# Attention and gated FFN on one core: where q's squares are transposed and summed, and three shifts in the order of work

## The reference

```python
xn = (x - mean) / sqrt(var + 1e-5)
q = rmsnorm(xn @ Wq.T) * q_norm_w      # 32 heads of 128
k = rmsnorm(xn @ Wk.T) * k_norm_w      # 8 groups of 128, 4 heads each
v = xn @ Wv.T
scores = q @ k.T / sqrt(128) + slope[h] * (s - t)   # causal, masked above the diagonal
s = concat_heads(softmax(scores) @ v) @ Wo.T
f = (silu(xn @ gate) * (xn @ up)) @ down            # hidden size 1792
# gate, up, down: integers, (w - zero) * scale per 128 rows
out = x + s * silu(f)
```

## Time and profile before

| | |
|---|---|
| three runs | 1301.31, 1301.42, 1301.54 us; median 1301.42 |
| the profiled execution | 1302.0 us, its span 1300.2 us |
| granted TensorE clock | full (2.4 GHz level) in all 40 slices |
| PE busy | 1281.2 us, 99% of the span |
| DVE busy | 972.3 us, 75% |
| POOL busy | 711.4 us, 55% |
| ACT busy | 650.8 us, 50% |
| DMA | 62.08 MB, mean 48 GB/s |

### The profile page before, as it was taken

How to read it: one execution, slowest core, us unless ns; L and a number is a source line. 1 busy time by engine, 2 the same in 40 slices (tenths; PEclk the granted TensorE clock), 3 DMA queues, 4 the chain that set the end, 5 groups by cost and what they waited for, 6 DMA issues and landing times.

```text
span 1300.2 us, 21057 instructions
## 1 busy us (share of the span) xinstructions
PE 1281.2 (99%) x7141; PEld 1099.9 (85%) x7141; DVE 972.3 (75%) x2089; ACT 650.8 (50%) x1433; POOL 711.4 (55%) x758
## 2 busy tenths in 40 slices
PE   8999999999999999999999999999999999999998
PEld 7888888888888888888888888888888888888887
DVE  6555555578888777877787778777877787778887
ACT  4322222355565555555555555555555555555552
POOL 4855555535555455545554555455545554555486
PEclk9999999999999999999999999999999999999999
DMA  6554555110010000000100000001000000000211
GB/s 187 160 143 130 128 129 130 31 74 17 17 34 17 17 18 33 18 17 17 33 18 17 17 33 17 17 17 34 17 17 18 33 17 17 17 17 17 98 57 66
DMA packets 31965, 62.08 MB, mean 48 GB/s; under 512 B 3840, under 2 KB 4096, under 8 KB 31744
## 3 DMA queue, kind: packets, MB, share of 16 engines
q1 hardware_dynamic: 31872, 60.88, 16.2%
HBM read 56.67 MB, written 4.19 MB: 47 GB/s over the span
## 4 chain that ended last, share of the span: by engine, by line
PE 89%; DVE 6%; ACT 2%; issue 2%; POOL 1%; DMA 0%; DVEq 0%; POOLq 0%
PE O L1088 31%; PE O L1149 13%; PE S L1668 12%; PE T L1109 10%; PE S L1128 5%; PE S L1131 5%; PE S L1129 5%; DVE pb L840 2%; PE T L1171 2%; PE O L1682 1%; PE T L1682 1%; PE O L1684 1%; PE T L1684 1%; PE O L1683 1%; PE T L1683 1%
## 5 line engine op out<-in xcount | busy, mean ns | idle before, releaser
L437 POOL TENSOR_TENSOR pb<-rel,coef 128x1024 f32<-128x1024 f32 (+7 forms) x256 | 293.2, 1160 | 139.9 <-PE T L1109 134.6
L579 ACT ACTIVATE pb<-pb,low 128x1024 f32<-128x1024 f32 (+7 forms) x256 | 198.9, 777 | 182.4 <-DVE low L840 180.5
L569 ACT ACTIVATE pt_h<-T 128x512 fp32r<-128x512 f32 (+3 forms) x384 | 185.0, 486 | 119.0 <-PE T L1109 115.8
L824 DVE TENSOR_TENSOR pt_l<-T,pt_h 128x512 fp32r<-128x512 f32 (+3 forms) x384 | 209.7, 549 | 43.1 <-ACT pt_h L569 43.0
L840 DVE CUSTOM_DVE_ANT_0 pb<-S,pb,ninv 128x1024 f32<-128x1024 f32 (+7 forms) x256 | 207.4, 810 | 36.8 <-PE S L1131 31.9
L1109 PE MATMUL T<-ident,pb 128*128 128x128 f32 x1152 | 188.9, 273 | 10.6 <-DVE ssum L869 4.7
L849 DVE TENSOR_SCALAR pb<-pb,rinv 128x1024 f32<-128x1024 f32 (+7 forms) x256 | 174.5, 682 | 9.0
L1109 PEld LDWEIGHTS T<-ident,pb 128*128 128x128 f32 x1152 | 140.5, 140 | 47.9 <-issue 13.9
L1128 PE MATMUL S<-kT_h,q_h 128*128 128x512 f32 (+2 forms) x384 | 141.5, 369 | 0.0
L1149 PE MATMUL O<-pt_h,v_h 128*128 128x512 f32 (+2 forms) x384 | 140.7, 366 | 0.1
L414 POOL TENSOR_TENSOR inv<-ms,cst 128x4 f32<-128x4 f32 x64 | 76.3, 1192 | 112.3 <-DVE ms L872 112.3
(11 more groups left out here) (177 smaller groups left out, 2899.3 us busy)
## 6 DMA issues: line engine op xcount, KB each, us to landing
wq_in<-in_wq SPq DMA_DIRECT2D x32, 256.0 KB, 2.8
wo_in<-in_wo SPq DMA_DIRECT2D x32, 256.0 KB, 2.6
stage<-in_wkv SPq DMA_DIRECT2D x8, 512.0 KB, 4.4
pb<-in_gate_w SPq DMA_DIRECT2D x14, 256.0 KB, 2.7
pb<-in_gate_z SPq DMA_DIRECT2D x14, 256.0 KB, 3.6
pb<-in_gate_s SPq DMA_DIRECT2D x14, 256.0 KB, 5.1
pb<-in_up_w SPq DMA_DIRECT2D x14, 256.0 KB, 5.3
pb<-in_up_z SPq DMA_DIRECT2D x14, 256.0 KB, 6.2
```

The costliest lines, as they stand in the source:

```text
L437: g_.tensor_tensor(pbuf(idx, t), rel[:, TOK - w:TOK], coef[:, t:t + 1].to_broadcast([P, w]), ALU.mult).then_inc(bias_ready, 1)
L569: a_.activation(pt_lot(pt_h, t, n), bank[:, 0:m * P].rearrange("p (k w) -> p k w", w=P), ACT.Copy).then_inc(tr_hi, 1)
L579: a_.activation(pbuf(idx, t), pbuf(idx, t), ACT.Exp, bias=low[:, idx:idx + 1], scale=-1.0, accum_out=rsum[:, idx:idx + 1]).then_inc(exps_r ...
L824: v_.tensor_tensor(pt_lot(pt_l, t, n), bank[:, 0:m * P].rearrange("p (k w) -> p k w", w=P), f(pt_lot(pt_h, t, n)), ALU.subtract).then_inc( ...
```

## The change

Half 0's squares no longer take part in the turns of the transpose banks.

- For heads 1 to 31, PE transposes them into the first bank of S[0] (`SQ_BANK`) with `squares_of_half_0`, which waits for q's squares and for logits 0 of this head (`logits_ready >= 8h + 1`), and raises a semaphore of its own, `sq_tr`. DVE's `mean_sq0` sums from there and raises `sq_sum`. Scores 2 gets a second wait, for `sq_sum`. The place among PE's work is the same.
- `PARTS` has 13 parts, and the bank of a part is that of its running number (`part_bank`).
- In the first and the last group, at j = 1 to 3, DVE sums in front of q_lo, not behind it. At j = 0 and in the steady groups the sum keeps its place.
- In heads 0 and 1, q_lo of the next head's qc1 moves behind the low part (4,1) and logits 5.
- In the prologue the transposes of x's tiles 6 and 7 stand in first_kv(4), not in first_kv(5).
- SP's wait in head 31 is for `sq_tr`.

```diff
-PARTS = ["ss0"] + LOTS[:LOTS.index((3, 0))] + ["ss1"] + LOTS[LOTS.index((3, 0)):]
-LN_PARTS = QT + 1
+PARTS = LOTS[:LOTS.index((3, 0))] + ["ss1"] + LOTS[LOTS.index((3, 0)):]
+LN_PARTS = QT + 2
+def part_bank(part):
+    return (part + 1) % 2
...
+    SQ_BANK = S[0][:, 0:CH]
...
-                    sp.wait_ge(tr_ready, part_no(h, "ss0") + 1)
+                    sp.wait_ge(sq_tr, h)
...
-            bank = T[place_in_head(h, (t, n)) % 2]
+            bank = T[part_bank(part_no(h, (t, n)))]
...
+        def mean_sq0(h):
+            cs = slice(0, CT)
+            dve.wait_ge(sq_tr, h)
+            v_.tensor_reduce(out=ssum[:, cs], in_=SQ_BANK.rearrange("p (k w) -> p k w", w=P),
+                             axis=mybir.AxisListType.X, op=ALU.add).then_inc(sq_sum, 1)
+            dve.wait_ge(sq_sum, h)
             v_.tensor_scalar(ms[:, cs], ssum[:, cs], HD * RMS_EPS, None, ALU.add).then_inc(ms_ready, 1)
...
                 if j > 0:
                     normalise(h, 0)
                     logits(h, 1)
+                    if kind != "steady":
+                        mean_sq0(h)
                     q_lo(at, f"qc0_{j}")
...
-                if prev:
-                    mean_sq(h, 0, part_no(h, "ss0"), T[0])
+                if prev and (j == 0 or kind == "steady"):
+                    mean_sq0(h)
                 normalise(h, 1)
...
                 normalise(h, 4)
-                if kind == "first" and not w:
-                    q_lo(at, f"qc1_{nx}")
                 lot(h, 4, 1)
                 if w and more and kind != "steady":
                     project(at, f"w2_{j}", 4 + j % 2, kind == "first")
                 logits(h, 5)
+                if kind == "first" and not w:
+                    q_lo(at, f"qc1_{nx}")
                 normalise(h, 5)
...
+            if idx == 2 and h > 0:
+                pe.wait_ge(sq_sum, h)
             bank = S[idx % 2]
...
+        def squares_of_half_0(at, h, j):
+            pe.wait_ge(out_hi, at.hi(f"qc0_{j}"))
+            pe.wait_ge(logits_ready, h * QT + 1)
+            for k in range(CT):
+                ins = nc.tensor.transpose(SQ_BANK[:, k * P:(k + 1) * P], sq[:, k * P:(k + 1) * P], ident[:, :])
+            ins.then_inc(sq_tr, 1)
...
-        first_kv(4, (False, True))
-        first_kv(5, (False, True), (6, 7))
+        first_kv(4, (False, True), (6, 7))
+        first_kv(5, (False, True))
...
                 def squares0(h=h, j=j):
-                    squares(at.hi(f"qc0_{j}"), 0, part_no(h, "ss0"), T[0])
+                    squares_of_half_0(at, h, j)
```

More of the change, by code:

```diff
@@ L86 @@
 LOTS = [(t, n) for t in TILES for n in range(len(parts(t)))]
-PARTS = ["ss0"] + LOTS[:LOTS.index((3, 0))] + ["ss1"] + LOTS[LOTS.index((3, 0)):]
-LN_PARTS = QT + 1
-assert len(PARTS) % 2 == 0
+PARTS = LOTS[:LOTS.index((3, 0))] + ["ss1"] + LOTS[LOTS.index((3, 0)):]
+LN_PARTS = QT + 2
 def place_in_head(h, key):
@@ L251, in attention @@
     tr_ready, tr_hi, tr_lo = sem("tr_ready"), sem("tr_hi"), sem("tr_lo")
+    sq_tr, sq_sum = sem("sq_tr"), sem("sq_sum")
     out_ready, out_hi, out_free = keep["out_ready"], sem("out_hi"), keep["out_free"]
@@ L871, in mean_sq @@
             dve.wait_ge(tr_lo, part + 1)
+            v_.tensor_scalar(ms[:, cs], ssum[:, cs], HD * RMS_EPS, None, ALU.add).then_inc(ms_ready, 1)
+        def mean_sq0(h):
[4 more added lines that the diff above has]
+            dve.wait_ge(sq_sum, h)
             v_.tensor_scalar(ms[:, cs], ssum[:, cs], HD * RMS_EPS, None, ALU.add).then_inc(ms_ready, 1)
@@ L924, in _ @@
         mean_sq(0, 1, QT, T[1])
-        mean_sq(0, 0, part_no(0, "ss0"), T[0])
+        mean_sq(0, 0, QT + 1, T[0])
         dve.wait_ge(kt_hi, 2)
@@ L1015, in group @@
                 if more:
-                    mean_sq(h + 1, 1, part_no(h, "ss1"), T[place_in_head(h, "ss1") % 2])
+                    mean_sq(h + 1, 1, part_no(h, "ss1"), T[part_bank(part_no(h, "ss1"))])
                 logits(h, 6)
@@ L1106, in lot @@
             pe.wait_ge(tr_lo, no - 1)
-            bank = T[place_in_head(h, (t, n)) % 2]
+            bank = T[part_bank(no)]
             for k in range(m):
@@ L1275, in rest_of_first_head @@
             squares(pro.hi("qc1_0"), 1, QT, T[1])
-            squares(q0_hi, 0, part_no(0, "ss0"), T[0])
+            squares(q0_hi, 0, QT + 1, T[0])
         gate_up, y_units, steps = feed.pe(pe)
@@ L1282, in _ @@
         gate_up(0, 1, 0, first=True)
-        pe.wait_ge(tr_lo, LN_PARTS + 1)
+        pe.wait_ge(tr_lo, LN_PARTS)
         pe.wait_ge(out_free, pro.n("qc1_0"))
@@ L1365, in squares1 @@
                 def squares1(h=h, nx=nx):
-                    squares(at.hi(f"qc1_{nx}"), 1, part_no(h, "ss1"), T[place_in_head(h, "ss1") % 2])
+                    squares(at.hi(f"qc1_{nx}"), 1, part_no(h, "ss1"), T[part_bank(part_no(h, "ss1"))])
                 now = [f"kv{j}"] * (kind == "steady")
```

## The result

The changed kernel took **1294.53 us** (median of 6 runs, 1294.28 to 1294.79) against 1301.37 us (6 runs) of the kernel before on the same chip: 6.84 us less, ratio 0.9947, 95% interval 0.9937 to 0.9957. The forecast was 1295.0 us. The profiled execution took 1294.79 us with a span of 1293.0 us.

A forecast was written before the change was run, and what follows sets the result against it. TensorE's queue, busy 99% of 1300.2 us, was taken as the bound, so only its standstills could be won. 3.1 + 1.4 + 1.2 + 0.7 = 6.4 us gave a median of 1295.0 us, own range 1294.0 to 1296.8, 8-in-10 range 1293.0 to 1298.2.

The forecast's parts named there:

- (a): Squares of half 0 into the score bank: 0.26 us in each of 12 odd steady heads, 3.1 us; even heads 0.
- (b): Sum in front of q's low part, first and last group: 0.8 + 0.3 + 0.3 us in heads 1, 3, 29, 1.4 together.
- (c): q's low part behind logits 5 in heads 0 and 1: 0.6 us each, 1.2 together.
- (d): Prologue, x's last transposes one half-unit sooner, removing a wait for their low part: 0.7 us.
- (e): Banks alternating over 13 parts and 31 extra semaphore waits on TensorE: taken as 0, bounded by 0.9 us.
- R1: Wait only moves: third score tile waits for the sum in steady heads; 1298.1 us, chance 0.16.
- R2: More is kept: DVE's chain gets shorter with the sum first, heads 2, 3, 29, 30; 1292.4 us, chance 0.12.
- R3: Slower: the sum takes longer from the score bank; 1312 us if twice as long, chance 0.03.
- R4: Next to nothing: standstills at (a) and (c) are replaced at once by others no row shows; 1300 us, chance 0.05.

The follow-up runs named there:

- E4: The changed kernel with (a) alone undone, half 0's squares back in the shared transpose banks with 14 parts: 1297.94 us.
- E5: The changed kernel with v0's low part in front of normalise 1 on DVE in heads of even j: 1293.08 us.
- E8: The changed kernel with v0's low part in front of normalise 1 at j = 0 alone: 1292.28 us, ratio 0.9932.
- E3: The changed kernel with the order of (b) alone undone, the sum behind q's low part but read from the score bank: 1294.70 us.
- E6: The changed kernel with DVE's sum behind normalise 1 in steady heads and at j = 0 of the last group: 1311.09 us, ratio 1.0074.
- E7: E5, and at j = 0 DVE's order logits 0, logits 1, normalise 0, sum, q's low part: 1295.60 us.
- E9: E5 plus one small GpSimd multiply in front of k's norm at j = 2 of groups 0 to 6: 1292.11 us.
- E10: E9, but with the changed kernel's order at j = 2 in the first and last group: 1291.54 us, ratio 0.9924.
- E1: The changed kernel with (d) alone undone, x's last transposes back in first_kv(5): 1295.32 us.

## Why the prediction was right

**(a) Right, a little small.** 3.4 us against 3.1: the twelve heads keep 0.28 us each, not 0.26. E4, where this alone is undone, loses 3.1 us in them; the rest of its 3.41 is mostly head 1's 0.27, which belongs to the bank too. Even heads gain nothing, held at w0, as forecast; E5 and E8 confirm the holder, since taking 0.6 us out of DVE's chain in front of w0 brings 0.3 us at once in heads with j = 0.

**(b) The size right (1.38 against 1.4), the booking wrong.** The step booked 0.8 + 0.3 + 0.3 to the sum's order. E3 shows that order and bank overlap: with the bank alone heads 3 and 29 gain all of theirs and head 1 0.41; with the order alone (E4) 0.28, 0.25 and 0.61. Only head 1 needs both, and the 1.0 us that I said the bank alone would give there is 0.41. What was right is the cap: 0.30 us of slack up to the first lot of tile 5 in the earlier trace rows, read as the most that head 29 can keep, gave 0.24, and the release at 303.77 in head 1 follows its normalise and one low part, as worked out.

**(c) Right.** 1.17 us in the traces for 1.2, 0.92 between medians.

**(d) Mis-sized.** I took 0.7 us, between the bounds of 0.60 and 0.75. It is 0.79 between medians (0.90 if each is taken against the kernel before beside it) and 0.95 in the traces from the place of the edit on. The wait itself was 0.77, the upper bound. The other 0.18 us come behind first_kv(6): 0.07 by first_kv(7) and most of the rest by the FFN's first unit. I gave that nothing; what it waits for there was not traced.

**(e) Right at 0.** The odd steady heads show it: with the new wait in front of their scores the stretch takes 0.79 us, as in head 0, which has no such wait. Even heads could not show it, since the hold at w0 would cover it. My bound was slightly off: 0.26 - 0.24 is 0.02, not 0.03, so 0.6 us and not 0.9.

**Head 31** was forecast to gain nothing, and the end came 0.2 us sooner there. E3 and E4 have it too (0.18 and 0.20), so it hangs on neither of the two alone; what does bring it stays open. That the forecast gave it nothing is a miss of 0.2. Its first lot of tile 4 starts 0.15 us sooner against the squares, although I had it bound by a chain that does not shorten.

**The sum and the range.** The terms came to 6.4 us and the traces have 7.2, nearly every miss on the same side: 0.25 for (d), 0.3 for (a), 0.2 for head 31, and 0.1 by which the start ran ahead before any edit. The median moved by 6.84, and the forecast was 0.5 us too high. The lower end of the forecast's own range, 1294.0, does not follow from what it names ((d) at 0.76 and (b) by 0.3 give 1294.6); the measured 1294.53 lies just outside that, and inside the wider 1293.0 to 1298.2.

**The rivals.** R1 fell for the steady heads: the margin of 0.12 us was 0.11 and held in all. E6 shows it was a rival with a real price: with the sum 0.6 us later the scores wait in 25 heads, and the kernel is 16.6 us slower than the changed one. The rule of the Trainium skill (Perfetto Trace Analysis, section Optimizing Tensor Performance) that independent groups rotate through banks would have had it likely. Here scores 0, squares and scores 2 follow in one bank and it costs nothing, since the sum is done 0.11 us before it is due. In E3 and E6, where it is not, the bank does stop TensorE. R2 (a shorter chain on DVE keeps more) fell: heads 2 and 30 gained 0. R3 fell with the sum's 0.68 to 0.69 us from the score bank, R4 with the list of waits.

**Where I did go wrong is E7.** Its step "normalise 0 comes 0.4 us sooner" took DVE's order for its time: an instruction taken out of an idle stretch shortens nothing, and put behind it lengthens the chain. The second half of the loss, the long multiply, I had in no text before E9. That GpSimd's place caused it in E7 is read from the same pattern of rows (656.00 before 656.07) and was not tried by itself.

## What to carry to other kernels

When an engine reads 99% busy, compare the start-to-start distance of the same stretch between two places where it should be equal; 0.26 us per head, 3.4 us in all, stood in no list of waits. A gain ends at the next thing that is due: look for the slack of that one before you add up, and give a removed wait no more than this slack. Of two changes that remove the same wait, each alone may bring all of it, so undo them one by one. And before you move work on DVE, look which GpSimd instruction starts within some 0.1 us of each of its fast multiplies.

## What the runs showed of the hardware

- **A pair of DVE and GpSimd instructions is a matter of who is first.** The same 128x640 multiply took 0.55 us or 1.33 us, as it began 0.12 us before or 0.05 us after GpSimd's 1.04 us one. The same held in all six steady heads with j = 2, once with GpSimd ahead by less than 0.01 us. One more instruction of 0.20 us on GpSimd made the heads concerned faster (E9, E10).
- **The lag from DVE's end to TensorE's start** was 0.15 us at every low part and sum in the rows above (head 12's w0, heads 0 and 29, E6's scores), but 0.06 us where a lot waited for the normalise's multiply (head 14 of E5: 718.74 + 1.33 = 720.07 to 720.13). The low parts and sums read PSUM, the multiply reads and writes SBUF; that this is the reason was not tested.
- **The start of an execution varies.** In the ten kernels with the same prologue the squares started 33.40 to 33.86 us into the span, and the two with the old one (E1 and before) differed by 0.61 us, all in places that no edit touched. Little of it is made up later: untouched heads mostly agree within 0.05 us. Edits of this size are better read by head, from the place of the edit on, than from one pair of times.
